# Attention's division moved from VectorE to ScalarE (a copy) and GpSimd (inverse by power, one Newton step, product)

## The reference, cut to what matters

```python
weights = softmax(q @ k.T * scale (+ mask), axis=-1)
out = weights @ v            # per head, 8 wide
y = x + concat(out) @ Wo.T
```

## Time and profile before

| | |
|---|---|
| median of three runs | 1010.62 us (1009.87 to 1011.01) |
| span of the profiled execution (first to last instruction) | 1007.3 us |
| around the span, against the median | 3.3 us |
| TensorE, VectorE, ScalarE, GpSimd busy | 88%, 76%, 65%, 39% of the span |
| granted clock of TensorE, mean | 0.968 |

### The profile page before, as it was taken

One profiled execution on the slowest core, in us unless ns is written; L12 is line 12 of the kernel. 1 busy time (PEld: TensorE's weight loads), 2 busy tenths in 40 slices (PEclk: granted clock), 3 DMA queues, 4 the chain that ended last, 5 costly groups with the idle time before them and its releaser, 6 DMA issues.

```text
span 1007.3 us, 22853 instructions
## 1 busy us (share of the span) xinstructions
PE 883.9 (88%) x9093; PEld 447.3 (44%) x9098; DVE 764.2 (76%) x1156; ACT 654.5 (65%) x1285; POOL 390.2 (39%) x607
## 2 busy tenths in 40 slices
PE   7999999998878888888988678889989999999983
PEld 5778777787633443334562222236322222222232
DVE  4667766856587677887667498786889999999855
ACT  2555565655526777785546548775768988998881
POOL 3755767778332551124454211352341112111340
PEclk8999999999899999998998899999999999999996
DMA  8000000200501034111420601033106000100000
GB/s 299 1 2 1 1 1 2 75 1 1 151 1 41 22 131 139 39 39 49 133 75 2 202 21 40 4 98 105 52 2 202 21 20 20 30 11 2 4 23 22
DMA packets 49407, 52.53 MB, mean 52 GB/s; under 512 B 8875, under 2 KB 40619, under 8 KB 49141
## 3 DMA queue, kind: packets, MB, share of 16 engines
q1 hardware_dynamic: 45012, 48.12, 15.6%
q0 software_dynamic: 4288, 2.94, 1.1%
HBM read 32.37 MB, written 19.68 MB: 52 GB/s over the span
## 4 chain that ended last, share of the span: by engine, by line
PE 49%; DVE 29%; ACT 7%; issue 5%; DMA 4%; POOL 3%; SPq 2%; DVEq 0%; ACTq 0%; POOLq 0%
DVE arena L1956 21%; PE banks L1618 9%; PE banks L1583 7%; PE banks L1503 5%; ACT arena L1776 3%; PE banks L759 3%; PE banks L485 3%; PE banks L495 2%; PE banks L1693 2%; PE banks L1701 2%; DMA arena<-arena 2%; PE banks L654 2%; PE banks L754 1%; PE banks L716 1%; PE banks L705 1%
## 5 line engine op out<-in xcount | busy, mean ns | idle before, releaser
L1776 ACT ACTIVATE arena<-banks 128x512 f32<-128x512 f32 (+1 forms) x768 | 409.1, 587 | 115.3 <-PE banks L1583 81.9
L1956 DVE TENSOR_REDUCE arena<-banks 128x2 f32<-128x1024 f32 (+1 forms) x384 | 440.1, 1198 | 56.3 <-PE banks L1503 29.1
L1618 PE MATMUL banks<-arena 128*9 128x256 f32 (+1 forms) x3328 | 252.6, 379 | 7.4 <-ACT arena L1789 4.6
L1503 PE MATMUL banks<-arena 56*128 56x512 bf16 (+3 forms) x896 | 163.3, 366 | 31.8 <-DVE arena L1956 25.2
L1583 PE MATMUL banks<-arena 61*128 61x512 bf16 (+4 forms) x896 | 165.5, 369 | 28.7 <-ACT arena L1776 20.9
L1583 PEld LDWEIGHTS banks<-arena 61*128 61x128 bf16 (+1 forms) x896 | 44.7, 93 | 185.3 <-ACT arena L1776 155.5
L1357 POOL CAST arena<-arena 16x128 bf16<-16x128 f32 x32 | 8.9, 279 | 296.2 <-ACT arena L1844 292.3
L1618 PEld LDWEIGHTS banks<-arena 128*9 128x9 f32 x3328 | 51.9, 89 | 130.7 <-issue 82.4
L1503 PEld LDWEIGHTS banks<-arena 56*128 56x128 bf16 x896 | 45.2, 95 | 57.1 <-DVE arena L1956 44.6
L383 POOL TENSOR_TENSOR arena<-arena 128x8 f32<-128x8 f32 (+1 forms) x35 | 51.3, 1467 | 30.7 <-DVE arena L2120 28.3
L1367 POOL DMA_DIRECT2D arena<-arena x96 | 55.1, 577 | 10.7 <-POOL arena L1360 9.2
(11 more groups left out here) (243 smaller groups left out, 1460.5 us busy)
## 6 DMA issues: line engine op xcount, KB each, us to landing
arena<-k_products SPq DMA_DIRECT2D x32, 224.0 KB
arena<-q_products SPq DMA_DIRECT2D x64, 112.0 KB
q_products<-arena SPq DMA_DIRECT2D x16, 384.0 KB, 3.4
k_products<-arena SPq DMA_DIRECT2D x16, 384.0 KB, 3.8
arena<-e_w SPq DMA_DIRECT2D x22, 256.0 KB, 3.3
arena<-arena POOLq DMA_DIRECT2D x96, 4.0 KB, 1.8
sorted_rows<-c_pads SPq DMA_DIRECT2D x2, 709.5 KB, 8.5
arena<-sorted_rows SPq DMA_DIRECT2D x4, 258.0 KB, 3.0
```

Source lines behind the costliest of these rows:

```text
L1503: ins = nc.tensor.matmul(bank(first + par)[:, at:at + hi - lo], Qs[k_][rows, qc, y, qo:qo + P], Ks[k_][rows, y, lo:hi], start=True, stop=n ...
L1618: ins = nc.tensor.matmul(PS[h * VROWS:h * VROWS + VW, AV_BANK, o:end], V[:, b, kt, HG * g + h, :], Pr[u % PROBS][:, h, o:end], start=(kt = ...
L1776: s_.activation(Pr[s % PROBS][:, 2 * x + par, o:C], scores[:, o:C], ACT.Exp) \
L1956: v_.tensor_reduce(of[:, :, x], two_banks[:, :, 0:width], AX.X, ALU.max).then_inc(ring_dve, 1)
```

## The change

ScalarE copies the nine columns of each head out of the turned bank into one of two new buffers `oq`. GpSimd raises the sums to the power -1, makes one Newton step (three operations on 16 columns) and multiplies the eight columns by the result into `On` (five instructions, four of them with a `link`; once more a memset of -1). VectorE does nothing for `O` any longer. The bank of `O` is given back by ScalarE, and `N` on TensorE waits for GpSimd's product (`o_divided`) where it waited for VectorE's.

```diff
-        rden = A.tile(NT // 2, HG)
+        oq = [A.tile(QT, HG, VW) for _ in range(2)]
+        rden, dtmp, minus = A.tile(QT, HG, 1), A.tile(QT, HG, 1), A.tile(1)
...
-        BY_ACT, BY_BOTH = "M H x k q Ta T0 Q QS lat KL K KS V0".split(), "h"
+        BY_ACT, BY_BOTH = "M O H x k q Ta T0 Q QS lat KL K KS V0".split(), "h"
...
+                    elif kind == "O":
+
+                        n, c = divmod(k, 2)
+                        g = n % NG
+                        taken(pool, "O", k)
+                        ready(pool, o_divided, k)
+                        if g == 0 and n >= NG:
+                            taken(pool, "N", (n // NG - 1, c))
+                        dst = On[:, QT * c:QT * (c + 1), HG * AD * g:HG * AD * (g + 1)]
+                        den = oq[k % 2][:, :, :, AD:]
+                        if k == 0:
+                            link(g_.memset(minus, -1.0))
+                        link(g_.tensor_tensor(rden, den, minus.unsqueeze(1).unsqueeze(1).to_broadcast([P, QT, HG, 1]), ALU.pow))
+                        link(g_.tensor_tensor(dtmp, den, rden, ALU.mult))
+                        link(g_.tensor_scalar(dtmp, dtmp, -1.0, 2.0, ALU.mult, ALU.add))
+                        link(g_.tensor_tensor(rden, rden, dtmp, ALU.mult))
+                        g_.tensor_tensor(dst.rearrange("p t (h e) -> p t h e", h=HG), oq[k % 2][:, :, :, 0:AD],
+                                         rden.to_broadcast([P, QT, HG, AD]), ALU.mult).then_inc(o_divided, 1)
...
-                        taken(pe, "O", 2 * (NG * (b + 1) - 1) + c)
+                        pe.wait_ge(o_divided, 2 * (NG * (b + 1) - 1) + c + 1)
...
+                    elif kind == "O":
+
+                        act.wait_ge(ring_full, place[kind, k] + 1)
+                        ready(act, o_divided, k - 1)
+                        s_.activation(oq[k % 2].rearrange("p t h e -> p (t h) e"),
+                                      bank(ring_bank(place[kind, k])).rearrange("p (x e) -> p x e", e=VROWS)[:, :, 0:VW],
+                                      ACT.Copy).then_inc(ring_act, 1)
...
-                    elif kind == "O":
-                        n, c = divmod(k, 2)
-                        g = n % NG
-                        o4 = bk.rearrange("p (t h e) -> p t h e", t=QT, h=HG)
-                        link(v_.reciprocal(rden, o4[:, :, :, AD]))
-                        dst = On[:, QT * c:QT * (c + 1), HG * AD * g:HG * AD * (g + 1)]
-                        v_.tensor_tensor(dst.rearrange("p t (h e) -> p t h e", h=HG), o4[:, :, :, 0:AD],
-                                         rden.unsqueeze(3).to_broadcast([P, QT, HG, AD]),
-                                         ALU.mult).then_inc(ring_dve, 1)
-                        taken(dve, "O", k)
```

More of the change, by code:

```diff
@@ L994, in build @@
         o_copied, mx_ready, m_split = sem("o_copied"), sem("mx_ready"), sem("m_split")
+        o_divided = sem("o_divided")
         e_picked, e_placed, e_steered, e_biased = (sem("e_" + k) for k in ("picked", "placed", "steered", "biased"))
```

## The result

1029.22 us median (1025.85 to 1030.8, 4 runs) against 1010.82 us for the kernel before (4 runs): ratio 1.0178, 95% interval 1.0151 to 1.0206, so 18 us slower. Forecast were 1022.2 us, 11.6 us more, in a range of 1013 to 1037: the direction and the range held, the size was 7 us too small. The profiled span is 1026.9 us, 19.6 more than before.

A forecast was written before the change was run, and what follows sets the result against it. It took the chain through VectorE's division and TensorE's scores as the bound, with GpSimd's queue deciding the cost. Terms -4.8 + 0.8 + 1.9 + 2.2 + 0.5 + 5.2 + 5.8 = +11.6 on 1007.3, plus 3.3: 1022.2 us, range 1013 to 1037.

The forecast's parts named there:

- GpSimd's chain of 4.3 us: GpSimd's power, three small operations, product and four links in each block's division: 4.3 us, ends 3.0 and 5.6.
- ScalarE's copy costs nothing: ScalarE's copy of 144 columns out of PSUM, 0.3 us a block, lies in an idle hole of 0.65 us.
- 0.28 us gained a division: Next VectorE reduction starts 0.28 us sooner, not 0.58, waiting for TensorE's scores; 17 divisions on the chain give 4.8 us.
- Mask rows just in time: Second layer's split runs 2.2 us late behind GpSimd's division, using up the slack; 0.1 us for each of eight steady blocks.
- Late splits of blocks 20 and 29: Splits behind these divisions on GpSimd, whose mask rows TensorE waits for, come later still: +1.9 and +2.2 us.
- The tail, 5.2 + 5.8: The last two N, (3, 0) and (3, 1), wait for GpSimd's divisions of blocks 30 and 31: +5.2 and +5.8 us.
- norm and first N, +0.5: Block 8's division delays the norm before a root on GpSimd by 0.4 us; a first N just late adds 0.1.

The follow-up runs named there:

- the copy alone: Changed kernel, but VectorE does every whole division out of ScalarE's copy and GpSimd none; ratio 1.0024 to the kernel before.
- e2: Changed kernel, but VectorE divides blocks 1, 20, 29, 30 and 31 out of ScalarE's copy; ratio 0.9992 to the kernel before.
- the longer chain: Changed kernel with GpSimd's power done twice in blocks 21 to 28; 1071.83 us in one run, beside 1016.37 for the kernel before.

## Why the prediction was right, point by point

- **GpSimd's chain of 4.3 us.** Right, each term within 0.05 us. The slope from 4 to 8 columns of the power carried to 16. The Trainium skill (GPSIMD Engine Reference, section 3.1) has elementwise work on GpSimd at about twice VectorE's time. The product took 1.4 times VectorE's, 0.41 us for 0.29, which is on the near side of that; the power took nearly 12 times the reciprocal's, 2.93 us for 0.25. The upper end of this sum is mis-added in the prediction: its terms give 5.8 us, not 5.6.
- **ScalarE's copy costs nothing.** Right in the second layer, shown by the copy alone. In the first layer not settled, at most some 5 us by the interval.
- **0.28 us gained a division, because TensorE fills the bank late.** Right at the place: the reduction waits 0.28 us for the scores. In the second layer it is near the mark too: 13 of the 17 divisions lie behind the first scores of block 16, and the version that leaves 12 of them off VectorE (`e2`) is 3.0 us shorter there, for 12 x 0.28 = 3.4. The versions in which VectorE keeps the reciprocal gain 1.6 to 2.9. In the first layer no gain is shown beyond the spread, and in the changed kernel itself the late mask rows take it back from block 23 on.
- **Mask rows just in time.** Right: from landing to first scores 2.2 us before and 0.13 to 0.15 after in six of the eight steady blocks (blocks 24 and 25 keep 1.8 and 0.6), and level from block 23 to 30. It was as close as it reads: these first scores start as soon as their rows land, and every further us of chain was paid, as the longer chain shows.
- **Late splits of blocks 20 and 29.** Right in place, 1.9 and 2.2 us forecast. The last split did start 2.3 us later behind block 30's first scores, but that cost 1.2 us: its third DMA took 1.7 us to land where it took 2.9 before, which nothing in the forecast foresaw. From block 21 to 23 it was 4.2: the wait, and 2.2 us of half clock.
- **The tail, 5.2 + 5.8.** Right for the waits: 5.5 for the first, and for the second 6.8 + 1.3 to the end with, of these, 2.6 of clock. (Half clock in the last us is nothing new, the kernel before has it from 991 us on; the changed kernel has it from the wait on.) The chain that ended last, after: start us, us, what.

```profile
974.69 0.78 POOL arena L1445
975.47 2.90 POOL arena L1382
...
979.90 1.09 PE banks L1653 x4
...
1000.96 2.86 POOL arena L1382
...
1005.35 1.10 PE banks L1653 x4
```

- **What was off** is the size of two terms. First, the prediction priced each wait by its length and took TensorE to go on as before; the clock after the waits added 4.8 us. Second, "norm and first N, +0.5" were the only places counted in the first layer, and the largest was missed: +3.8 us at block 4. There the division of block 1 stands in front of the latents' root and the rotation on GpSimd, ScalarE's own queue waits for that rotation, and TensorE for ScalarE. First ScalarE's copy in the kernel before, without a wait, then the kernel after:

```profile
353.16 0.63 ACT L568 ACTIVATE arena<-arena 128x512 bf16<-128x512 f32 x1
```

```profile
354.29 1.32 POOL L463 TENSOR_TENSOR arena<-arena 128x512 f32<-128x512 f32 x1
355.64 0.63 ACT L569 ACTIVATE arena<-arena 128x512 bf16<-128x512 f32 x1 [3.69 <-POOL arena L463]
356.18 1.07 ACT L1796 ACTIVATE arena<-banks 128x512 f32<-128x512 f32 x2
...
356.82 0.60 PE L1603 MATMUL banks<-arena 59*128 59x512 bf16 x2 [4.12 <-ACT arena L1796]
```

Taking block 1 back on VectorE gave 2.4 of the 3.8 us back. The other 1.3 are not the change's: from block 3 to 4 the kernel before took 24.1 us in its first profile, at a granted clock of 1.00, and 25.4 in its second, at 0.93, as the version with block 1 on VectorE did (25.5, 0.93). The changed kernel took 27.9, at 0.88.

So against the forecast of 11.6 us the landmarks, counted from block 1, have 20.0: 4.8 for the clock after the three waits and 3.8 at block 4, 0.8 in small differences of the other terms, less the 1.0 that the last split cost less than forecast. That makes 8.4 us. Direction and places were no luck, as the experiments took the loss back where it was forecast; that block 31's rows landed faster was, and so was the first profile's full clock at block 4, on the other side.

## What to carry to other kernels

Work moved to an engine that is idle 61% of the time is priced by its queue, not by its share: list what stands right behind each moved piece, who waits for that, and how much slack it has; here the loss was gone once five of 32 divisions were taken back, and four of these (20, 29, 30, 31) show it in landmarks that last. Look first where the chain is serial, at the tail, and for what stands in front of the moved piece as well. Waits of TensorE of 2.4 to 5 us cost more than their length here, because the matmuls after them ran at half clock for some us.

## What the runs showed of the hardware

- A power on GpSimd takes 1.04, 1.67 and 2.93 us for 4, 8 and 16 columns of 128 partitions, where a product takes 0.20 to 0.23: 0.16 us for each further column. VectorE's reciprocal of the 16 columns takes 0.25.
- In and after waits of 2.4 to 5 us TensorE's granted clock was at its lower level (0.50), for 3.4 to 6.8 us in the middle of the kernel, and to the end in the tail; with matmuls put in the wait it stayed at 1.00. A wait of 2.23 us, before block 22 in the kernel with the longer chain, was not followed by such a stretch.
- Stretches at the lower clock also come and go between profiles of one and the same kernel, and the chips differ by 8 us on it, at the two places where GpSimd issues indirect DMAs.
